# A two-layer mixture-of-experts kernel: the gated sums of one quarter of the condition move from VectorE to GpSimd

## What is computed

```python
x = x + L0_ffn(L0_cond(x, cond))   # recurrent net, then 31 routed experts (top 3) and a shared one
x = x + L1_ffn(L1_cond(x, time))   # four gated experts and a shared one, then 8 routed experts (top 2)
```

```python
for e in range(4):
    h = gelu(c @ ew1[e] + eb1[e])
    y = h @ ew2[e] + eb2[e]
    out = out + w_be[:, e][:, None, None] * mask[e][None, :, None] * y
shared = gelu(c @ sw1 + sb1) @ sw2 + sb2
return out + shared
```

## Time and profile before

| | us |
|---|---|
| three timed runs | 475.62, 482.92, 483.75 |
| median | 482.92 |
| the profiled execution, its own time | 472.43 |
| its span, first to last instruction | 470.7 |
| mean granted clock of TensorE, share of full speed | 0.906 |

### The profile page before, as it was taken

The page is one execution under the profiler, slowest core; times in us unless marked ns, Lnnn a source line. Parts: engine busy times, 40 slices in busy tenths (PEclk is TensorE's granted clock), DMA queues, the critical chain, the costliest instruction groups (busy, mean ns, idle before and its releaser), DMA issues.

```text
span 470.7 us, 7360 instructions
## 1 busy us (share of the span) xinstructions
PE 393.6 (84%) x2189; PEld 304.6 (65%) x2189; DVE 229.2 (49%) x704; ACT 215.2 (46%) x536; POOL 247.8 (53%) x279
## 2 busy tenths in 40 slices
PE   8997989988747499996999989657696899999850
PEld 7993344422447499784675686546484899998750
DVE  2679876323323266355376766954450344442210
ACT  2332345654322256872666486323163466665410
POOL 7198977777667400574770010375530067667734
PEclk9997899999867599998999989896789799999995
DMA  4770428752424234784720029311138546772343
GB/s 110 193 215 22 165 85 262 276 162 69 151 67 112 68 92 124 272 270 142 248 52 7 22 47 301 96 55 36 42 122 242 126 66 160 163 164 24 30 131 117
DMA packets 59324, 60.09 MB, mean 128 GB/s; under 512 B 11733, under 2 KB 46998, under 8 KB 58518
## 3 DMA queue, kind: packets, MB, share of 16 engines
q1 hardware_dynamic: 45318, 39.04, 27.8%
q0 software_dynamic: 9200, 10.50, 11.3%
q10 hardware_dynamic: 4768, 10.09, 5.8%
HBM read 31.50 MB, written 21.42 MB: 112 GB/s over the span
## 4 chain that ended last, share of the span: by engine, by line
PE 56%; DVE 13%; issue 10%; DMA 9%; another core or an unknown queue 4%; ACT 3%; POOL 3%; POOLq 0%; ACTq 0%; DVEq 0%
PE ps L1938 7%; PE ps L1927 6%; DMA out_d<-ysb,xrow_a 5%; PE ps L2052 5%; PE ps L2002 4%; PE ps L2014 4%; PE ps L1800 3%; PE ps L2230 3%; PE ps L1801 3%; PE ps L1802 3%; DMA out_dram<-ysb,xrow_a 2%; PE ps L2158 2%; PE ps L1987 2%; PE ps L2247 2%
## 5 line engine op out<-in xcount | busy, mean ns | idle before, releaser
L1115 ACT ACTIVATE hid<-ps,cols 128x512 f32<-128x512 f32 (+3 forms) x84 | 51.6, 618 | 52.6 <-PE ps L2052 17.0
L932 POOL DMA_INDIRECT ygat<-yd,idxy x36 | 39.2, 1088 | 48.3 <-ACT hid L1115 38.6
L949 POOL DMA_INDIRECT disp<-stage,idx x28 | 28.5, 1016 | 36.4 <-DVE idx L1645 24.5
L977 POOL DMA_INDIRECT out_dram<-ysb,xrow_a x16 | 24.9, 1559 | 40.6 <-DVE ysb L1785 35.9
L1800 PE MATMUL ps<-in_hi,wc 128*128 128x512 f32 (+3 forms) x84 | 43.0, 511 | 3.4 <-DVE in_lo L1500 2.4
L2247 PE MATMUL ps<-wf,hid 128*128 (+1 forms) x344 | 42.9, 277 | 2.4 <-issue 1.1
L2247 PEld LDWEIGHTS ps<-wf,hid 128*128 128x128 f32 x344 | 40.4, 192 | 4.0 <-issue 3.9
L1024 ACT ACTIVATE hid<-ps,cols 128x512 f32<-128x512 f32 x35 | 23.9, 687 | 39.2 <-PE ps L1927 16.7
L1196 ACT ACTIVATE hid<-ps,b1d 128x128 f32<-128x128 f32 x108 | 30.6, 382 | 21.3 <-PE ps L2230 15.3
L1927 PE MATMUL ps<-h_f,raw 128*128 128x512 f32 x70 | 39.2, 646 | 0.9 <-ACT hid L1024 0.8
L1938 PE MATMUL ps<-yg,raw 128*128 128x512 f32 x62 | 33.8, 634 | 4.0 <-DVE yg L1417 3.6
(11 more groups left out here) (320 smaller groups left out, 913.7 us busy)
## 6 DMA issues: line engine op xcount, KB each, us to landing
disp<-empty ACTq DMA_DIRECT2D x14, 616.5 KB
g0a<-gt_d SPq DMA_DIRECT2D x6, 1280.0 KB
w1d<-wf SPq DMA_DIRECT2D x27, 256.0 KB, 2.5
yd<-yr SPq DMA_DIRECT2D x33, 128.0 KB
wf<-in_L_ffn_w_dram SPq DMA_DIRECT2D x1, 2048.0 KB, 8.7
wf<-in_L_ffn_w_dram SPq DMA_DIRECT2D x8, 256.0 KB, 7.2
raw<-in_L_ffn_We_dram SPq DMA_DIRECT2D x2, 960.0 KB, 7.2
xrow_a<-disp SPq DMA_DIRECT2D x24, 68.5 KB, 2.0
```

Source lines behind the costliest of these rows:

```text
L932: G.indirect_dma_start(out=ygat[:, i, k, :], out_offset=None, in_=yd, in_offset=bass.IndirectOffsetOnAxis(ap=idxy[:, i, k:k + 1].bitcast(U ...
L977: G.indirect_dma_start(out=(out_rows, out2)[h % 2], out_offset=bass.IndirectOffsetOnAxis(ap=xrow(h // 2)[:, h % 2, D:D + 1].bitcast(U32), ...
L1115: A.activation(hid[:, n % 4, lo:hi], src, ACT.Gelu_apprx_tanh, bias=bias).then_inc(s_hid, 1)
```

## The change

Of the eight parked units VectorE keeps five: 1 to 4 after items 56 to 59 and 10 after item 61 (before: 65). GpSimd does units 6, 7 and 8, one after the other, behind the memset of `b2diag` and before the scatters: for each a multiply and an add, every operation waiting for the one before. It waits for the gates and for `s_ev` to reach 12, that is for the eviction of units 0 to 11. The semaphore `s_b2z` is renamed `s_pg`: 1 after the memset, 2 after the last add. `tokens(1)` waits for this instead of `s_c`; `s_c` now counts four groups. The last add of quarter 1 is now that of unit 14, after item 63.

```diff
+BY_POOL = [u for u in DEFER if UNITS[u][1] == _b]
+LAST_OF = [max(u for u in DEFER if UNITS[u][1] == _a), max(u for u in range(NU) if UNITS[u][1] == _c), NU - 3, NU - 1]
-LAST_OF = [max(u for u in DEFER if UNITS[u][1] == q) for q in (_a, _b, _c)] + [NU - 3, NU - 1]
...
-GATED_AT = dict(zip((56, 57, 58, 59, 61, 62, 64, 65), DEFER))
+GATED_AT = dict(zip((56, 57, 58, 59, 61), [u for u in DEFER if u not in BY_POOL]))
...
-            sp.wait_ge(s_b2z, 1)
+            sp.wait_ge(s_pg, 1)
...
-            G.memset(b2diag[:], 0.0).then_inc(s_b2z, 1)
+            G.memset(b2diag[:], 0.0).then_inc(s_pg, 1)
+            pool.wait_ge(s_gcT, 1)
+            pool.wait_ge(s_ev, FIRST_GATED)
+            for u in BY_POOL:
+                e, q, a, b = UNITS[u]
+                got, to = late(u)[:, a:b], c_f[:, q * C0 + a:q * C0 + b]
+                by_time = got.rearrange("p (t b) -> p t b", b=B)
+                link(G.tensor_tensor(by_time, by_time, gc_T[:, e - 1, :].unsqueeze(1).broadcast_to([P, (b - a) // B, B]),
+                                     ALU.mult))
+                add = G.tensor_tensor(to, to, got, ALU.add)
+                if u == BY_POOL[-1]:
+                    add.then_inc(s_pg, 1)
+                else:
+                    link(add)
...
-                pe.wait_ge(s_c, g + 1)
+                if g == 1:
+                    pe.wait_ge(s_pg, 2)
+                else:
+                    pe.wait_ge(s_c, g if g else 1)
...
-                    pe.wait_ge(s_c, NG)
+                    pe.wait_ge(s_c, NG - 1)
```

More of the change, by code:

```diff
@@ L526, in build @@
         s_gcT = sem("s_gcT")
-        s_b2z = sem("s_b2z")
+        s_pg = sem("s_pg")
         s_gexp = sem("s_gexp")
```

## The result

| | before | changed |
| --- | --- | --- |
| median of 4 runs | 479.27 us (473.95 to 483.75) | 482.74 us (478.39 to 485.34) |
| profiled execution | 472.43 us, span 470.7 | 481.03 us, span 479.3 |
| ratio | | 1.0305, interval 1.0224 to 1.0386 |

Forecast were 482.2 us and no measurable change; the comparison says slower. The ratio leaves out executions over 1.5% above the fastest of their own kernel (482.92 and 483.75 of before, none of the changed), while the medians are over all of them and stand at 482.74 / 479.27 = 1.007. Without those two the values of the record give 482.74 / 474.79 = 1.017; where the rest of the 1.0305 comes from they don't show.

The account below looks back on a forecast made before the run. Bound: TensorE up to 291.24 us, VectorE from 291.26 to 302.42. A 1.5 us loss less a 2.17 gain gives -0.7: profiled 472.43 to 471.7, median 482.92 to 482.2, range 473 to 486.5.

Parts of the forecast that it names:

- Part 1: VectorE, items 61 to 64: less parked work, so group 1's logits begin at 300.30 instead of 302.47, 2.17 us gained.
- Part 2: GpSimd behind the memset of `b2diag`: six operations of about 1.3 us; the scatters behind them covered by 10 us.
- Rival A: First quarter: GpSimd waits, VectorE runs at 0.72 a step, all the gain stays: -2.2 us, 470.3; chance 0.2.
- Part 3: First quarter: VectorE and GpSimd hold each other off, 0.96 per GpSimd operation; VectorE 4.9 late, group 0's logits 1.5.
- pair: One VectorE and one GpSimd operation in alternation: 1.68 us, where VectorE alone takes 0.72.
- cover: VectorE's wait of 3.41 us ahead of the copy to `lgf`, set against its 4.9 us delay.
- Rival B: Logits of group 0: longer hold, over 1.07 us per GpSimd operation; +1.1 (473.5), at most +2.7 (475.1); chance 0.2.
- The Trainium skill's rule: VectorE's two-SBUF-input operations against GpSimd's SBUF reads: the first issuer fully blocks the other; taken literally, +1.1 us.
- the bounds I had given: Net effect: -2.2 us if GpSimd always gives way, +2.7 if its three multiplies run at the comparison's rate.
- Part 4: Semaphores: quarter 1's release moves from item 65 to 63, its taker being TensorE's item 73; worth nothing.
- rival C: Unexplained chain stalls at 310.95 (4.94) and 319.00 (5.70): one falls away or is added, about 5 us either way; chance 0.15.
- I carry the shift to the end: Behind group 1's logits nothing waits for a clock of its own, so the net -0.7 us reaches the end.

Follow-up runs that it names:

- one-input work: Kernel before, with six one-input scalings of 128x512 added on GpSimd, on spare memory behind its memset, chip 12: 427.03 us.
- only the collision: Kernel before, VectorE keeping all eight parked units, GpSimd adding six operations of the same form on spare memory, chip 14: 485.63 us (470.93 to 492.65).

## Why the prediction was right and wrong

**Part 1, right.** Forecast was that group 1 follows group 0 by 2.17 us less. It is 27.45 - 15.25 = 12.20 before and 26.94 - 17.01 = 9.93 after: 2.27. Group 1's logits begin directly behind `hid_lo`, with no wait for GpSimd.

**Part 2, right.** Six operations, 1.26 to 1.31 where they met nothing and 1.6 where they did; the first scatter comes 13.68 us behind them and waits for `idx`, not for them. Rival A is out: GpSimd doesn't give way.

**Part 3, mechanism and pair right, its cover mis-sized.** A pair takes 1.67 to 1.71; the quarter is 4.97 late (forecast 4.9) or 5.64, by the phase of the memset. Rival B needs 1.07 or more per GpSimd operation; 4.97 / 6 is 0.83 over six and 0.99 over the five operations that were held, so the longer hold is out. The Trainium skill's rule ("SBUF — State Buffer", "Who interferes with whom") is borne out for two-input operations as blocking, and the trace stays as much milder as forecast: 1.68 and not 1.98 for a pair. What failed is "The cover is the wait of 3.41 us ahead of the copy to `lgf`". I took it as a fixed slack. It held 1.6 us of TensorE's half clock a few microseconds before. It is also mis-sized by 0.2 in itself: I took the start of group 0's logits from the chain (290.44), where the timeline has 290.27, so the delay by my own sum is 1.7 and the net -0.5, and 1.76 and -0.51 were measured. Where that half clock comes, TensorE arrives 1.6 us later and the net is -0.5; where it does not, TensorE idles 3.82 us, and the next point applies.

**A term was missing.** In TensorE's idle 3.82 us the clock falls to 1.2 GHz for 6.8 us, and that costs 0.83 (10.75 against 9.92 from group 0 to group 1). My sum had put it at nothing. The first profile is then, against the first of before: +2.40 (group 0) - 2.27 (part 1) + 0.83 (clock) = +0.96. Against a kernel before that also lacks the early half clock (group 1 at 25.9, in the runs without scatters on chip 14 and with one-input work) it is 28.43 - 25.9 = +2.5. So the effect on this stretch is -0.5 to +2.5 us by the clock's state, inside the bounds I had given (-2.2 to +2.7), though my value was its favourable end. The first profile's +0.96 is near the +1.1 of rival B, but by another mechanism.

**Part 4, right.** Quarter 1's release, which group 2 takes, was two items earlier, and no wait for it stands ahead of group 2's logits before or after.

**The total, wrong, and at the step on scatter.** The prediction put 0.87 on a change within 2%, by "the executions alone from 472.4 to 483.8" and by rival C with "about 5 us either way". Those were 4 values. The same code shows 472.4 to 490.8 on chip 14 and 423.7 to 436.7 on chips 4 and 12; the waits of rival C are there in all profiles of the one and in none of the other, and the scatters bring those of the router. That the gathers bring the ones ahead of the change is a guess by this and wasn't tried.

The measured 1.0305 is 14.6 us, and no term of the stretch comes near: 9.66 us of the profiled difference lie ahead of the changed code, and the table ends with the changed kernel 1.1 us ahead. The two later pairs of profiles end the other way, 7.5 us (chip 14) and 2.8 us (chip 4) behind. On chip 4 this arises long behind group 4: in the 60 us from 110 behind zero on, TensorE waits 2.7 us for `ysb`, and 1.6 in the kernel before. Three pairs don't tell whether the change has a part in it. The three comparisons of the two kernels say 1.031, 1.010 and 0.989, and the interval of the last excludes the other two, though its 4.9 us gained are no more in the stretch (-0.51) than the 14.6 lost; their medians over all runs say 1.007, 1.011 and 1.003. The 3% is therefore not shown to be the change's. Where it comes from stays open. What is shown is a small loss or gain in the stretch, and medians that lean to slower by less than the scatter.

That "I carry the shift to the end" holds isn't shown either: multiplies alone gained 2 to 3 us at the routers' last group on chip 12 and nothing in the total, while leaving the units out, 4.1 us early at group 4, gave 0.988. And the median of 482.74 beside a forecast of 482.2 is luck: the forecast was laid on a median of three, 482.92, that a fourth execution moved to 479.27. What takes a shift of 2 us up behind the router is open; so is whether code length or place moves the waits upstream, and why only some chips have them.

## What to carry to other kernels

Before work is moved to an engine that stands idle, ask what both engines then do at the same time: two engines with two-input operations on SBUF alternate, and each moved operation here cost the engine that it relieved 0.96 us, more than the 0.72 it saved; moving the multiplies alone, ahead of the memset, kept the gain at group 1, though no total showed it. VectorE's other operations can be held as well: a copy of 128x8 waited 1.02 us. A slack read from one trace may be made of a low clock that isn't there next time, so look at the granted clock ahead of the wait before you spend it. And where executions of equal code scatter over 18 us, count from a common event just ahead of the change: it shows tenths where the total shows nothing. What it shows holds for the stretch, and has to be followed to the end before it is called a gain.

## What the runs showed of the hardware that was not expected

- GpSimd operations with one input of 128x512 took 10.30 us for six beside VectorE, and cost it only 0.3 at a meeting (0.98 or 1.06 instead of 0.69), 1.05 us over six, against about 1 us each for two inputs.
- VectorE's copy of 128x8, one input, lasted 1.19 us instead of 0.17 beside GpSimd's two-input add.
- In an idle time of TensorE of 3.82 us the clock fell to 0.50 for 6.8 us, in both profiles that have such a wait; in the wait in which 16 matmuls of 64 columns ran it stayed at 1.00. Behind an idle time of 1.58 (only the collision) it stayed at 1.00 for the 12 us that follow, and behind one of 1.59 (changed kernel, chip 4) it fell 2.1 us after the logits had begun, for 3.4 us.
- The same program takes 428 to 429 us on two chips and 475 to 482 on others. The difference goes with waits that no engine of the core explains, but they are 20.2 us of the chain in the first profile, less than half of it; with 28 scatters of GpSimd taken out, those of the router went, and groups 1 to 4 took 26.7 us instead of 41 to 43, as on the chips without such waits (26.7 with the scatters in).
